# Attention and a ternary projection on one core: transposes of two units change places with slices of the projections

## The chip, the cores and the metric

The kernel runs on one core of a Trainium2 chip. The time is the device time in microseconds (us). The kernel before took 2060.3 us, the median of three runs (2057.4, 2060.3 and 2060.49). The profiled execution took 2057.48 us, of which the trace spans 2055.7 us.

The engines are named as in the profile: PE (the matrix engine, with its weight loads as PEld), DVE (the vector engine), ACT (the scalar engine), POOL (GpSimd) and SP (which issues the DMAs).

## The reference, cut to what matters

```python
# x: (8, 512, 1024) f32; 16 heads of 64; cond_1: (8, 1)
q, k, v = proj(x, Wq), proj(x, Wk), proj(x, Wv)       # (b, 16, 512, 64)
q = q * minimum(cond_1, 4.0)
scores = einsum('bhqd,bhkd->bhqk', q, k) / sqrt(64)
scores = where(causal, scores, finfo.min)
attn = softmax(scores)
out = einsum('bhqk,bhkd->bhqd', attn, v)
y = out.reshape(b, s, 1024) @ Wo.T
# ffn: weight rounded to -1, 0, 1 times alpha; y rounded to 8 bits by row
return x + absmax_act(y) @ ternary_weight(weight).T + bias
```

## The kernel before, in words

There are three stages. The first computes V for all batches (to about 345 us), the second does the attention (to about 1600 us), the last multiplies by Wo, quantises, and does the ternary product. The change lies in the second.

**Steps.** The 16 heads form 4 groups of 4. One step handles one batch and one group, so there are 32 steps, group by group, 8 batches each. A step projects Q and K of its 4 heads and does 16 units of attention: a unit u is one head and one tile of 128 queries (`h, qt = divmod(u, 4)`). By the causal mask the unit has only `(qt + 1) * 128` keys, so a unit is 128, 256, 384 or 512 wide in turn, and unit 5 has two 128-column blocks, unit 6 has three.

**The operands' precision.** Each f32 operand of the projections is kept as a high and a low part in fp32r. The x slices are split so: ACT writes the high part (`x_high`, L359), and the low part (`x_low`, L365) is computed by DVE for even slices k and by POOL for odd ones. A projection slice J(gi, k) is three matmuls of 512 columns (L174) and, for gi = 0, first waits until slice k's low part is there. gi is 0 to 3: K and Q of heads 0 and 1, then K and Q of heads 2 and 3.

**One unit's way.** S(u): two score matmuls on PE (L242, L243). M(u): DVE adds the mask and finds the row minimum (L254). E(u): ACT takes the exponential and the row sum (L261). I(u): DVE inverts the sum (L267). Then POOL normalises (L273). T(u): PE transposes `qt + 1` blocks into one of two `t_ps` banks (L283). H(u): ACT copies out the high part (L297). L(u): DVE the low part (L304). PV(h): eight matmuls with V for a head's four units (L317), which need the L of its last unit. T(u) waits for two things: that unit u is normalised, and that L(u - 2) has emptied its bank.

**The order.** Nothing is scheduled by a program: `pe_step`, `act_step`, `dve_step`, `pool_step` and `sp_step` each write out by hand what their engine does in a step. The attention of a step runs into the next: in these lists S(6) and later, and T(3) and later, are units of the step before (`old`), while J is of the present one (`now`). The head of a list is called a step's boundary here. There, ACT and DVE first empty the bank of the last projection, J(3) of the step before (`evac_hi`, `evac_lo`), and split the last x slices, 4 to 7. DVE does this in the order evac_lo(3), scale (L375), I(5), M(6), x_low 4, L(3), I(6), M(7), x_low 6, L(4), I(7). POOL does: normalise 5, x_low 5, normalise 6, normalise 7, x_low 7, normalise 8. ACT does H(6) directly ahead of V(0), the emptying of J(0)'s bank.

**Where old and now are both there.** This holds for 31 boundaries. In the first step there is no old, and after the last step there is no now.

**Group changes.** At three steps SP also loads the weights of the next group, behind the next x and ahead of the swapped copy of K, `k_sw` (L229, L230), that S(0) needs. In the step after each of these, ACT and DVE split one more piece of the weights at the boundary (L408, L398).

Of the kernel before, what the change touches and what calls it, by code (L numbers as in the profile page):

```python
# [36 lines left out]
def adaln_ffn_kernel(nc, x, xT, cond, wq, wk, wv, wo, wf, bias, out):  # L37
# [4 lines left out]
    with ExitStack() as ctx:  # L42
# [115 lines left out]
        def project(pe, it, g, gi, k):  # L158
            kind, n = groups[gi]
            bank = proj_ps[gi % 2]  # L160
            w = "kq".index(kind)
            if k == 0:

                if due(count := it * NEV + (EVAC[gi - 2] if gi >= 2 else EVAC[gi + NPROJ - 2] - NEV)):
                    pe.wait_ge(proj_lo_done, count)
                pe.wait_ge(wqk_lo_done, g * 4 + gi + 1)
            if gi == 0:
                pe.wait_ge(x_lo_done[k % 2], it * (KT // 2) + k // 2 + 1)
            col = slice(n * P, (n + 1) * P)
            out = bank[:, :]  # L170
            passes = [(w_lo[w][:, k, col], x_hi[:, k, :]), (w_hi[w][:, k, col], x_lo[:, k, :]),
                      (w_hi[w][:, k, col], x_hi[:, k, :])]
            for i, (l, r) in enumerate(passes):
                mm = pe.matmul(out, l, r, start=(k == 0 and i == 0), stop=(k == KT - 1 and i == 2))  # L174
            if gi == NPROJ - 1:

                mm.then_inc(x_free, 1)
            elif k == KT - 1:
                mm.then_inc(proj_done, 1)
# [52 lines left out]
        def scores(pe, it, u):  # L232
            h, qt = divmod(u, QT)
            n = it * UNITS + u
            if u % (2 * QT) == 0:
                pe.wait_ge(k_swapped[h // 2], (it + 1) * 32)
                pe.wait_ge(proj_lo_done, it * NEV + EVAC[h // 2 * 2 + 1])
            if due(count := n - 1):
                pe.wait_ge(max_done, count)
            w = (qt + 1) * P  # L240
            q = q_st[:, h, qt * P:(qt + 1) * P]
            pe.matmul(s_ps[u % 2][:, 0:w], q, k_sw[:, h, 0:w], start=True, stop=False)  # L242
            pe.matmul(s_ps[u % 2][:, 0:w], q, k_st[:, h, 0:w], start=False, stop=True).then_inc(s_done, 1)  # L243
# [32 lines left out]
        def transpose(pe, it, u):  # L276
            qt = u % QT
            n = it * UNITS + u
            pe.wait_ge(norm_done, n + 1)
            if due(count := n - 1):  # L280
                pe.wait_ge(pt_lo_done, count)
            for kb in range(qt + 1):
                mm = pe.transpose(t_ps[u % 2][:, kb * P:(kb + 1) * P], prob[:, u % 4, kb * P:(kb + 1) * P],  # L283
                                  ident[:, :])
            mm.then_inc(t_done, 1)
# [22 lines left out]
        def times_v(pe, it, h):  # L308

            pe.wait_ge(pt_lo_done, it * UNITS + (h + 1) * QT)  # L310
            pe.wait_ge(v_in[h], (it + 1) * 16)
            pe.wait_ge(o_sum_done[h % 2], it * NBLK + h // 2 + 1)
            for kb in range(QT):
                q0 = kb * P
                v = v_st[:, kb, h, :]
                for part in (pt_lo, pt_hi):
                    mm = pe.matmul(o_ps[h % 2][:, q0:S], v, part[h % 2][:, kb, q0:S],  # L317
                                   start=(kb == 0 and part is pt_lo), stop=(kb == QT - 1 and part is pt_hi))
            mm.then_inc(pv_done, 1)
# [172 lines left out]
        def attention_out(pe, t, p, half, k):  # L492
            first = isinstance(t, int) and t < 2
            if half == 0 and k == 0:
                pe.wait_ge(o_lo_done, t + 1)
                if not first:
                    if due(count := t - 1):
                        pe.wait_ge(y_free, count)
                elif t == 0:
                    pe.wait_ge(proj_lo_done, STEPS * NEV)  # L500
                else:
                    pe.wait_ge(max_done, STEPS * UNITS)
            if first and t == 0 and half == 0:
                pe.wait_ge(wo_lo_done, k + 1)
            w = slice(half * HALF, (half + 1) * HALF)
            o = slice(k * P, (k + 1) * P)
            for i, (a, b) in enumerate(((o_lo, wo_hi), (o_hi, wo_lo), (o_hi, wo_hi))):
                mm = pe.matmul(y_ps[p][half][:, :], a[p][:, o], b[k][:, w],  # L508
                               start=(k == 0 and i == 0), stop=(k == KT - 1 and i == 2))
            if k == KT - 1:  # L510
                mm.then_inc(y_done, 1)
# [674 lines left out]
        def pe_step(pe, old, now, nxt, qk_for=None, late_for=None, last=False):  # L1186
            o, n, g = old and old[0], now and now[0], now and now[1]

            def J(gi, *ks):
                if now:  # L1190
                    for k in ks:
                        project(pe, n, g, gi, k)

            def S(u):
                if u >= 6 and old:
                    scores(pe, o, u)
                elif u < 6 and now:
                    scores(pe, n, u)

            def T(u):  # L1200
                if u >= 3 and old:
                    transpose(pe, o, u)
                elif u < 3 and now:
                    transpose(pe, n, u)

            def PV(h):
                if old:
                    times_v(pe, o, h)

            def Y(t, half, *ks):  # L1210
                if last and not now:
                    for k in ks:
                        attention_out(pe, t, t, half, k)

            def YY(k):
                Y(0, 0, k)
                Y(0, 1, k)

            S(6)
            T(3)  # L1220
            J(0, 0, 1)
            YY(0)
            S(7)
            T(4)
            J(0, 2, 3)
            YY(1)
            S(8)
            T(5)
            J(0, 4, 5)
            PV(0)  # L1230
            J(0, 6)
            S(9)
            T(6)
            J(0, 7)
            J(1, 0)
            YY(2)
            S(10)
            T(7)
            J(1, 1, 2, 3)
            YY(3)  # L1240
            S(11)
            T(8)
            J(1, 4, 5)
            S(12)
            T(9)
            YY(4)
            PV(1)
            J(1, 6, 7)
            S(13)
            T(10)  # L1250
            J(2, 0, 1)
            YY(5)
            S(14)
            T(11)
            J(2, 2, 3)
            YY(6)
            S(15)
            T(12)
            J(2, 4, 5)
            if not old:  # L1260
                pe.wait_ge(v_sum_done, 4 * (PAIRS - PLAIN))
            S(0)
            T(13)
            YY(7)
            PV(2)
            J(2, 6)
            S(1)
            T(14)
            J(2, 7)
            J(3, 0)  # L1270
            Y(1, 0, 0, 1, 2)
            S(2)
            T(15)
            J(3, 1, 2)
            Y(1, 0, 3, 4)
            S(3)
            T(0)
            J(3, 3, 4)
            Y(1, 0, 5, 6, 7)
            S(4)  # L1280
            T(1)
            PV(3)
            J(3, 5, 6)
            S(5)
            T(2)
            J(3, 7)
# [329 lines left out]
        @block.tensor  # L1616
        def _(pe):
            v_pe(pe)
            pe.wait_ge(const_ready, CONSTS)
            program(pe, pe_step)  # L1620

            for k in range(KT):
                if k == KT // 2:
                    transpose_y(pe, 0, 0)
                attention_out(pe, 1, 1, 1, k)
            ternary(pe, 0, 0)

            def body(t, p):
                attention_out_half(pe, t, p, 0)
                transpose_y(pe, t - 1, 1 - p)  # L1630
                attention_out_half(pe, t, p, 1)
                ternary(pe, t - 1, 1 - p)

            pairs(pe, body)
            transpose_y(pe, TILES - 1, 1)
            ternary(pe, TILES - 1, 1)
# [81 lines left out]
```

## Time and profile before

| | |
|---|---|
| profiled execution | 2057.48 us |
| its span | 2055.7 us |
| median of three runs | 2060.3 us |
| PE busy | 1988.6 us (97%) |
| PEld busy | 1619.1 us (79%) |
| DVE busy | 1411.2 us (69%) |
| ACT busy | 1115.7 us (54%) |
| POOL busy | 872.2 us (42%) |

Busy is the time in which an engine had an operation under way. The matmuls overlap each other, so PE's share says how rarely it stood still and not how full it ran. In the attention stage a step takes 38.03 us in the steady part (from one q_scale operation to the next), and each boundary looks like the others to a few hundredths of a microsecond.

### The profile page before, as it was taken

Reading aid. Unit: us, or ns where it says so; the run is one execution under the profiler, and the core shown is the slowest. Engines: PE = TensorE matmul, PEld = TensorE weight load, DVE = VectorE, ACT = ScalarE, POOL = GpSimd, SP = SyncE. Lnnn points to the kernel's source line nnn. Section 1 sums busy time; section 2 is a strip of 40 time slices with the busy share of each in tenths; the row PEclk is TensorE's granted clock in tenths of the full one; section 3 lists DMA queues with packets and bytes.
Section 4 is the critical chain, followed back from the end, with each engine's and each line's share of the span. In section 5 each row is a group of like instructions: output and inputs, shape, how many; then the busy total and the mean of one; then the engine's idle time right before and its main releaser. Section 6 shows DMA issues by size and latency. Waiting matters only on the chain.

```text
span 2055.7 us, 34723 instructions
## 1 busy us (share of the span) xinstructions
PE 1988.6 (97%) x10074; PEld 1619.1 (79%) x10074; DVE 1411.2 (69%) x3277; ACT 1115.7 (54%) x2497; POOL 872.2 (42%) x816
## 2 busy tenths in 40 slices
PE   8999999999999999999999999999998999999998
PEld 6888887888877888877888877888886777777775
DVE  6667776777777777778777777777776645545454
ACT  4554445777777777777777777777774000000000
POOL 0344333444435444435445435445443544444442
PEclk9999999999999999999999999999999999999999
DMA  6676645533543533543533543533553432333322
GB/s 204 225 232 219 203 170 183 156 112 114 141 149 103 159 107 105 155 148 103 151 115 102 158 149 103 154 112 102 158 153 101 130 120 94 107 108 100 114 92 82
DMA packets 200981, 282.43 MB, mean 137 GB/s; under 512 B 11216, under 2 KB 146384, under 8 KB 199760
## 3 DMA queue, kind: packets, MB, share of 16 engines
q1 hardware_dynamic: 200384, 281.07, 44.9%
q8 instruction: 34, 0.56, 0.1%
q10 hardware_dynamic: 528, 0.52, 0.1%
q14 instruction: 35, 0.29, 0.0%
HBM read 178.79 MB, written 69.21 MB: 121 GB/s over the span
## 4 chain that ended last, share of the span: by engine, by line
PE 47%; issue 27%; POOL 15%; DVE 5%; DMA 3%; ACT 2%; SPq 1%; POOLq 1%; DVEq 0%; ACTq 0%
POOL prob L273 9%; PE proj_ps L508 8%; PE s_ps L508 8%; PE t_ps L869 7%; PE proj_ps L174 6%; PE o_ps L869 6%; POOL parts L365 5%; PE o_ps L579 5%; DMA k_sw<-k_st 2%; PE o_ps L317 1%; PE t_ps L283 1%; DVE prob L254 1%; DVE parts L365 1%; PE t_ps L557 1%; PE s_ps L808 1%
## 5 line engine op out<-in xcount | busy, mean ns | idle before, releaser
L174 PE MATMUL proj_ps<-parts 128*128 128x512 f32 x3072 | 839.2, 407 | 6.0 <-POOL parts L365 3.6
L273 POOL TENSOR_TENSOR prob<-prob,row_inv 128x128 f32<-128x128 f32 (+3 forms) x512 | 383.1, 748 | 693.5 <-DVE row_inv L267 690.9
L174 PEld LDWEIGHTS proj_ps<-parts 128*128 128x128 f32 x3072 | 538.8, 189 | 112.1 <-POOL parts L365 13.3
L261 ACT ACTIVATE prob<-prob,row_min 128x128 f32<-128x128 f32 (+3 forms) x512 | 287.5, 561 | 145.8 <-DVE row_min L254 139.5
L254 DVE CUSTOM_DVE_ANT_0 prob<-s_ps,mask 128x128 f32<-128x128 f32 (+3 forms) x512 | 248.2, 485 | 56.5 <-PE s_ps L243 22.1
L297 ACT ACTIVATE pt_hi<-t_ps 128x128 fp32r<-128x128 f32 (+3 forms) x512 | 220.7, 431 | 112.2 <-PE t_ps L283 108.2
L564 ACT ACTIVATE yt_q<-t_ps 128x1024 bf16<-128x1024 bf16 x32 | 32.7, 1023 | 427.1 <-PE t_ps L557 427.1
L304 DVE TENSOR_TENSOR pt_lo<-t_ps,pt_hi 128x128 fp32r<-128x128 f32 (+3 forms) x512 | 249.0, 486 | 16.7 <-ACT pt_hi L297 12.5
L283 PE MATMUL t_ps<-ident,prob 128*128 128x128 f32 x1280 | 227.4, 276 | 31.9 <-DVE pt_lo L304 29.4
L365 POOL TENSOR_TENSOR parts<-x_raw,parts 128x512 fp32r<-128x512 f32 x128 | 183.4, 1434 | 18.1 <-ACT parts L359 18.1
L508 PE MATMUL proj_ps<-parts,o_parts 128*128 128x512 f32 x768 | 188.2, 400 | 2.6 <-issue 2.6
L283 PEld LDWEIGHTS t_ps<-ident,prob 128*128 128x128 f32 x1280 | 152.7, 141 | 47.5 <-issue 34.2
L508 PE MATMUL s_ps<-parts,o_parts 128*128 128x512 f32 x768 | 185.6, 397 | 0.0
L508 PEld LDWEIGHTS proj_ps<-parts,o_parts 128*128 128x128 f32 x768 | 143.7, 190 | 33.6 <-issue 3.0
L508 PEld LDWEIGHTS s_ps<-parts,o_parts 128*128 128x128 f32 x768 | 143.2, 189 | 30.7
L243 PE MATMUL s_ps<-k_st,q_st 128*128 128x128 f32 (+3 forms) x512 | 166.0, 324 | 0.0
L242 PE MATMUL s_ps<-k_sw,q_st 128*128 128x128 f32 (+3 forms) x512 | 158.3, 309 | 7.2 <-DMA k_sw<-k_st 7.0
L317 PE MATMUL o_ps<-pt_lo,v_st 128*128 128x512 f32 (+3 forms) x512 | 161.6, 326 | 2.7 <-DVE pt_lo L304 2.7
L359 ACT ACTIVATE parts<-x_raw 128x512 fp32r<-128x512 f32 x256 | 152.0, 618 | 3.1 <-DMA x_raw<-xT 2.2
L317 PE MATMUL o_ps<-pt_hi,v_st 128*128 128x512 f32 (+3 forms) x512 | 147.7, 325 | 0.0
L267 DVE RECIPROCAL row_inv<-row_sum 128x1 f32<-128x1 f32 x512 | 82.5, 161 | 92.9 <-ACT prob L261 85.6
L334 DVE TENSOR_TENSOR o_sum<-o_ps,o_low 64x512 f32<-64x512 f32 x128 | 87.4, 683 | 82.6 <-ACT o_low L326 82.5
(118 smaller groups left out, 2880.3 us busy)
## 6 DMA issues: line engine op xcount, KB each, us to landing
x_raw<-xT SPq DMA_DIRECT2D x128, 512.0 KB, 5.7
v_scratch<-v_out SPq DMA_DIRECT2D x64, 512.0 KB, 3.3
k_sw<-k_st SPq DMA_DIRECT2D x128, 256.0 KB, 4.7
v_st<-v_scratch SPq DMA_DIRECT2D x128, 256.0 KB, 4.2
oT_scratch<-o_sum SPq DMA_DIRECT2D x64, 256.0 KB, 2.5
x_raw<-oT_scratch SPq DMA_DIRECT2D x32, 512.0 KB, 4.8
x_tile<-x SPq DMA_DIRECT2D x32, 512.0 KB, 5.4
out<-res SPq DMA_DIRECT2D x32, 512.0 KB, 3.2
```

What stands on the lines that cost most here:

```text
L174: mm = pe.matmul(out, l, r, start=(k == 0 and i == 0), stop=(k == KT - 1 and i == 2))
L243: pe.matmul(s_ps[u % 2][:, 0:w], q, k_st[:, h, 0:w], start=False, stop=True).then_inc(s_done, 1)
L254: dve.tensor_tensor_reduce(prob[:, u % 4, 0:w], s_ps[u % 2][:, 0:w], mask[:, S - w:S], 1.0, -MASKED, ALU.add, ALU.min, row_min[:, u % 4:u ...
L261: act.activation(prob[:, u % 4, 0:w], prob[:, u % 4, 0:w], ACT.Exp, bias=row_min[:, u % 4:u % 4 + 1], scale=-1.0, accum_out=row_sum[:, u % ...
L273: pool.tensor_tensor(prob[:, u % 4, 0:w], prob[:, u % 4, 0:w], row_inv[:, u % 4:u % 4 + 1].broadcast_to([P, w]), ALU.mult).then_inc(norm_d ...
L283: mm = pe.transpose(t_ps[u % 2][:, kb * P:(kb + 1) * P], prob[:, u % 4, kb * P:(kb + 1) * P], ident[:, :])
L297: act.activation(pt_view(pt_hi[h % 2], qt), t_ps[u % 2][:, 0:(qt + 1) * P] .rearrange("p (k q) -> p k q", q=P), ACT.Copy).then_inc(pt_hi_d ...
L304: dve.tensor_tensor(pt_view(pt_lo[h % 2], qt), t_ps[u % 2][:, 0:(qt + 1) * P] .rearrange("p (k q) -> p k q", q=P), pt_view(pt_hi[h % 2], q ...
L317: mm = pe.matmul(o_ps[h % 2][:, q0:S], v, part[h % 2][:, kb, q0:S], start=(kb == 0 and part is pt_lo), stop=(kb == QT - 1 and part is pt_hi))
L365: eng.tensor_tensor(x_lo[:, k, :], x_raw[:, k, :], x_hi[:, k, :].bitcast(F32), ALU.subtract).then_inc(x_lo_done[k % 2], 1)
L508: mm = pe.matmul(y_ps[p][half][:, :], a[p][:, o], b[k][:, w], start=(k == 0 and i == 0), stop=(k == KT - 1 and i == 2))
L869: mm = pe.matmul(bank[:, :], xv[:, c, xp, ks], wv_view(c, wp)[:, k, :], start=(k == 0 and m == 0 and c not in (S2, S3)), stop=(k == CH - 1 ...
```

## The change

In the order of PE's step, the transposes of unit 5 move behind the projection slice J(0, 4), and those of unit 6 behind J(0, 7). Nothing is added and nothing is left out. The order of the other engines is not touched.

```diff
             S(8)
+            J(0, 4)
             T(5)
-            J(0, 4, 5)
+            J(0, 5)
             PV(0)
             J(0, 6)
             S(9)
+            J(0, 7)
             T(6)
-            J(0, 7)
             J(1, 0)
             YY(2)
```

PE's order around T(5), in the loop over the batches: the two rows with s_ps are S(8), t_ps is T, proj_ps is J (three matmuls a slice), o_ps is PV(0). Before:

```order
L242 MATMUL s_ps<-k_sw,q_st 128x128
L243 MATMUL s_ps<-k_st,q_st 128x128
L283 MATMUL t_ps<-ident,prob 128x128 x2
L174 MATMUL proj_ps<-parts 128x512 x6
L317 MATMUL o_ps<-pt_lo,v_st 128x512
```

And now:

```order
L242 MATMUL s_ps<-k_sw,q_st 128x128
L243 MATMUL s_ps<-k_st,q_st 128x128
L174 MATMUL proj_ps<-parts 128x512 x3
L283 MATMUL t_ps<-ident,prob 128x128 x2
L174 MATMUL proj_ps<-parts 128x512 x3
L317 MATMUL o_ps<-pt_lo,v_st 128x512
```

The three matmuls of J(0, 4) stand ahead of the two transposes of T(5); those of J(0, 5) stay behind them.

PE's order around T(6): the first proj_ps row is J(0, 6), then S(9), T(6), and J(0, 7) with J(1, 0). Before:

```order
L174 MATMUL proj_ps<-parts 128x512 x3
L242 MATMUL s_ps<-k_sw,q_st 128x256
L243 MATMUL s_ps<-k_st,q_st 128x256
L283 MATMUL t_ps<-ident,prob 128x128 x3
L174 MATMUL proj_ps<-parts 128x512 x6
L242 MATMUL s_ps<-k_sw,q_st 128x384
```

And now:

```order
L174 MATMUL proj_ps<-parts 128x512 x3
L242 MATMUL s_ps<-k_sw,q_st 128x256
L243 MATMUL s_ps<-k_st,q_st 128x256
L174 MATMUL proj_ps<-parts 128x512 x3
L283 MATMUL t_ps<-ident,prob 128x128 x3
L174 MATMUL proj_ps<-parts 128x512 x3
L242 MATMUL s_ps<-k_sw,q_st 128x384
```

J(0, 7) stands ahead of the three transposes of T(6), J(1, 0) behind them.

## Rows read from the trace of the kernel before

**Rows 1.** PE's waits over the whole span: engine, line, waited for: us in total, times, longest.

```profile
PE t_ps L283 <- DVE pt_lo L304: 29.4, 35, 2.8
...
PE s_ps L242 <- DMA k_sw<-k_st: 7.0, 3, 2.4
PE proj_ps L174 <- POOL parts L365: 3.6, 3, 1.2
```

**Rows 2.** Timeline of PE at one boundary: start, duration, operation, count, [idle before <- releaser].

```profile
973.38 0.41 PE L283 MATMUL t_ps<-ident,prob 128*128 128x128 f32 x2 [0.86 <-DVE pt_lo L304]
973.55 1.64 PE L174 MATMUL proj_ps<-parts 128*128 128x512 f32 x6
...
976.98 0.28 PE L242 MATMUL s_ps<-k_sw,q_st 128*128 128x256 f32 x1
...
977.22 0.49 PE L283 MATMUL t_ps<-ident,prob 128*128 128x128 f32 x3
977.78 1.67 PE L174 MATMUL proj_ps<-parts 128*128 128x512 f32 x6
```

**Rows 3.** Timeline of DVE at the same boundary.

```profile
971.94 0.69 DVE L365 TENSOR_TENSOR parts<-x_raw,parts 128x512 fp32r<-128x512 f32 x1
972.55 0.68 DVE L304 TENSOR_TENSOR pt_lo<-t_ps,pt_hi 128x512 fp32r<-128x512 f32 x1
...
973.82 1.28 DVE L365 TENSOR_TENSOR parts<-x_raw,parts 128x512 fp32r<-128x512 f32 x1
...
975.22 0.15 DVE L267 RECIPROCAL row_inv<-row_sum 128x1 f32<-128x1 f32 x1
...
977.23 0.68 DVE L334 TENSOR_TENSOR o_sum<-o_ps,o_low 64x512 f32<-64x512 f32 x1 [0.94 <-ACT o_low L326]
```

**Rows 4.** Timeline of POOL at the same boundary.

```profile
971.99 1.77 POOL L365 TENSOR_TENSOR parts<-x_raw,parts 128x512 fp32r<-128x512 f32 x1
...
975.45 1.04 POOL L273 TENSOR_TENSOR prob<-prob,row_inv 128x512 f32<-128x512 f32 x1 [0.90 <-DVE row_inv L267]
976.44 1.28 POOL L365 TENSOR_TENSOR parts<-x_raw,parts 128x512 fp32r<-128x512 f32 x1
```

**Rows 5.** Timelines of ACT, POOL and PE, behind T(6).

```profile
977.75 0.49 ACT L297 ACTIVATE pt_hi<-t_ps 128x384 fp32r<-128x384 f32 x1 [0.64 <-PE t_ps L283]
978.87 1.21 ACT L210 ACTIVATE k_st<-proj_ps 64x512 fp32r<-64x512 f32 x2 [0.63 <-PE proj_ps L174]
...
981.18 0.61 POOL L273 TENSOR_TENSOR prob<-prob,row_inv 128x256 f32<-128x256 f32 x1 [3.10 <-DVE row_inv L267]
...
984.28 0.41 PE L283 MATMUL t_ps<-ident,prob 128*128 128x128 f32 x2
```

**Rows 6.** Timeline of PE where T(10) stands among projections, no waits.

```profile
987.42 0.49 PE L283 MATMUL t_ps<-ident,prob 128*128 128x128 f32 x3
987.67 1.63 PE L174 MATMUL proj_ps<-parts 128*128 128x512 f32 x6
```

**Rows 7.** Timeline of PE, J(0,7) at a boundary behind a change of group.

```profile
939.75 1.66 PE L174 MATMUL proj_ps<-parts 128*128 128x512 f32 x6 [1.20 <-POOL parts L365]
```

**Rows 8.** PE at two group changes; then one stretch, its PEclk third from the end.

```profile
913.81 0.33 PE L242 MATMUL s_ps<-k_sw,q_st 128*128 128x128 f32 x1 [2.35 <-DMA k_sw<-k_st]
...
922.01 0.39 PE L242 MATMUL s_ps<-k_sw,q_st 128*128 128x512 f32 x1
...
1223.68 0.33 PE L242 MATMUL s_ps<-k_sw,q_st 128*128 128x128 f32 x1 [2.24 <-DMA k_sw<-k_st]
...
1230.29 0.39 PE L242 MATMUL s_ps<-k_sw,q_st 128*128 128x512 f32 x1
...
915.50:917.00 1.50, 1.50 (x6) 1.31 (x6) 0.41 (x1) 0.59 (x1) 0.40 (x1) 0.50 0.00 1
```

**Rows 9.** Timeline of PE at the last boundary, T(6) and J(0,7).

```profile
1513.42 0.49 PE L283 MATMUL t_ps<-ident,prob 128*128 128x128 f32 x3
1514.02 1.66 PE L174 MATMUL proj_ps<-parts 128*128 128x512 f32 x6
```

## The prediction

> **What bounds the kernel now.** I first read the page's busy shares: PE has work under way for 97% of the span, so time can be won or lost only where PE stands still, or where it is given more or less to do. The change gives it the same instructions. So I then read PE's waits for the whole span [rows 1]. The largest is T waiting for the low part L, 29.4 us in 35 waits, nearly one for each of the 31 boundaries. Two smaller ones matter too: the swapped K that S(0) needs, three times and at most 2.4 us, and the x slice that POOL splits, three times.
>
> The third view is PE's timeline at one boundary, with those of DVE and POOL beside it [rows 2 to 4]. Here the reader is to see two stops on PE. The first is open: T(5) idles 0.86 us, until L(3) ends on DVE (972.55 + 0.68 = 973.23, and T(5) starts at 973.38). The second is nearly hidden. T(6) starts at 977.22, and the next slice, J(0,7), at 977.78, 0.56 us later. Where nothing is awaited, the same three transposes let the next slice start after 0.25 us (987.42 to 987.67) [rows 6]. J(0,7) therefore lost 0.31 us, and the row prints no idle for it only because the last transpose was still draining. What it waited for is x_low 7 on POOL, which ends at 976.44 + 1.28 = 977.72, 0.06 us before J(0,7) starts. I compared all 31 boundaries: POOL's end is followed by J(0,7) after 0.05 to 0.06 us in each. At the last one T(6) and J(0,7) are 0.60 us apart [rows 9].
>
> **The change part by part.** *T(5) behind J(0,4).* J(0,4) needs x_low 4, which DVE ends at 971.94 + 0.69 = 972.63, so with the same 0.06 us it starts at about 972.7. T(5) had been idle from 972.52. A slice takes half of the 1.47 us in which the six matmuls of a pair are issued, 0.73 us. J(0,4) is through at 973.4, when T(5) could start anyway. So J(0,4) costs nothing: it fills most of the hole. J(0,5) then waits for x_low 5, which POOL ends at 971.99 + 1.77 = 973.76. It starts at 973.82, where it started at 973.55 + 0.73 = 974.28 before. PE is 0.46 us ahead, and J(0,5), PV(0), J(0,6) and S(9) come that much earlier. That x_low 6 is ready for J(0,6) is seen from its end on DVE, 973.82 + 1.28 = 975.10, ahead of the end of PV(0).
>
> *J(0,7) ahead of T(6).* Now PE comes to J(0,7) where T(6) would have been, at 977.22 - 0.46 = 976.76, and J(0,7) needs x_low 7, which is ready at 977.72. Can the 0.46 us move x_low 7? Its chain is normalise 7 on POOL (from 975.45, released by DVE), behind I(7) on DVE (975.22), behind x_low 6 (973.82 to 975.10), behind L(3) and x_low 4 [rows 3, 4]. Every link of it is a DVE or POOL operation that waits for no instruction that PE now issues sooner; DVE works through it without a stop after the emptying of J(3). It begins with the end of J(3,7), which the change does not touch. So I take x_low 7 to stay at 977.72 and J(0,7) at 977.78, with about 1.02 us of idle in front of it. All that the first part won is given back here.
>
> What differs is what stands behind the wait. Before, T(6) ran inside the time that PE had to wait for x_low 7 anyway. Now it runs after it, between J(0,7) and J(1,0). Before, J(1,0) started at 977.78 + 0.73 = 978.51; now T(6) starts there and J(1,0) 0.25 us later. The cost is the 0.25 us of [rows 6]. Its bounds: T(5)'s two transposes let the next slice start after 0.17 us, so three cost at least 0.24 us when a block is 0.085; at most it is the 0.49 us for which a group of three is recorded. I take 0.25, the same count of the same form, and keep 0.35 as a practical upper end, an estimate for the extra break in the matmul stream.
>
> *What waits for the later T(6).* It starts at 978.51 and not at 977.22, 1.29 us later. H(6) on ACT goes from 977.75 to 979.04, and V(0), queued behind it, from 978.87 to about 979.5, 0.6 us later [rows 5]. On DVE L(6), the low part of J(0)'s bank, and then I(9) and M(10) follow 0.6 us later, and on POOL normalise 9 goes from 981.18 to 981.8, ending at 982.4. PE needs that for T(9) at 984.28. There are nearly 2 us of cover, so this costs nothing. The swapped K leaves 0.6 us later as well, but S(0), which needs it, stands in the second half of the step.
>
> *How often.* The boundary occurs 31 times. In three of them the step loads the next group's weights and S(0) then idles 2.24 to 2.40 us for the swapped K [rows 1, 8]. That transfer queues behind the x and weight loads, which start when x_low 7 is done and keep the DMA engines full, so it does not move. There PE's extra 0.25 us disappears into the idle time. Left are 28 times 0.25 = 7.0 us. On the profiled execution's own 2057.48 us that gives 2064.5, and on the median of 2060.3 it gives 2067.3. The profiled execution is at the fast end of the runs shown; I take 2066, between the two.
>
> *The clock.* It adds spread. At the first and second group change the granted clock fell after the idle time; one stretch behind it is at 0.50, the 1.2 GHz level. At the third, after 2.24 us idle, it did not fall. From S(0) to S(3) the second took 922.01 - 913.81 = 8.20 us and the third 1230.29 - 1223.68 = 6.61, so one fall costs 1.6 us [rows 8]. The change shortens this idle to 2.0 to 2.15 us, which could save the two falls, 3.2 us. But at the boundary behind a group change, J(0,7) idled 1.20 us behind T(6) [rows 7]. With T(6)'s recorded 0.49 and the 0.4 won before it, that becomes about 2.1 us. Three of these could fall, 4.8 us. I count both at nothing in the sum and give them to the range. The Trainium skill (TensorE: Matmul & The Clock Gate, "What's actually happening") says that a gate sets the clock by how busy PE has lately been. The two falls agree with that. By it, the change's one stop of 1 to 2 us is more exposed than the two shorter ones that it replaces.
>
> **The rivals.** *It does what its form suggests: faster.* If x_low 7 were not what J(0,7) waits for, or moved forward with PE, J(0,7) would start at 976.76, J(1,0) at 976.76 + 0.73 + 0.25 = 977.74 instead of 978.51. That is 0.77 us, 28 times, 21.6 us: 2036 on the own time, 2039 on the median. It breaks even when x_low 7 ends 0.25 us earlier. For it speaks the 0.86 us idle at T(5), which J(0,4) really fills; against it, the 0.06 us between POOL's end and J(0,7), 31 times. 6%.
>
> *No difference.* The 7 us are there, but the shorter wait at the group changes keeps the clock up at two of them (-3.2), and nothing falls elsewhere: 2061.3 on the own time, 3.8 above it, which is inside what a measurement tells from nothing (0.2%, 4.1 us). Or some later wait that I read as zero takes up the 0.25 us. For it: the 2.24 us that passed without a fall. Against: J(0,7)'s 2.1 us has the same length. 12%.
>
> *Clearly slower.* POOL's x_low took 1.77 us in x_low 5 and 1.28 in x_low 7; during the former DVE's x_low 4 ran, which reads SBUF twice. Now OA(0) and M(9) move 0.46 us forward into x_low 7. If they slowed it by the same 0.49 us, J(0,7) would be later by that: 28 times 0.49 = 13.7 more, 2078 on the own time. Against it: OA(0) already ran beside x_low 7 (from 977.23 on) before, and x_low 7 took only its 1.28 us; OA(0) reads one of its inputs from PSUM. The Trainium skill (GPSIMD Engine Reference, "Key points") says that POOL shares SBUF interfaces with DVE and contends with instructions that have two SBUF inputs. By that rule x_low 4 slows POOL and OA(0) does not, as the rows have it. 5%.
>
> *My forecast,* 0.25 us in each of 28 steps, with falls of the clock going either way: 77%.
>
> **How the numbers follow.** Predicted 2066. The low end: the own time, 28 times 0.24 = 6.7, less 3.2 for two falls saved, 2061; I go to 2060 to take in part of the second rival. The high end: 2060.3, 28 times 0.35 = 9.8, and 4.8 for three new falls, 2074.9; I stop at 2074. The rest of the chance is outside. Slower by over 0.2%: the forecast and the third rival, 82%. Within 0.2%: 12%. Faster: 6%.
>
> **What would show it.** In the changed kernel's trace, T(5)'s wait for L(3) has gone or is below 0.1 us, and J(0,4) stands in its place. J(0,7) idles about 1.0 us, released by POOL's x_low, in 31 boundaries, so PE's waits show some 30 us there where they show 3.6 now. From the start of J(0,7) to J(1,0) it takes about 0.98 us, and a steady step 38.28 us and not 38.03. I am wrong if x_low 7 ends closer to J(3,7) than before, if the step is shorter than 38.0, or if a wait of PE appears that is in neither list, above all at T(9) or PV(1).

## The result, and the profile after

The changed kernel took 2069.84 us, the median of five runs (2066.54 to 2070.87), against 2060.3 us before. The ratio is 1.0045, with a 95% interval of 1.003 to 1.006. It is slower by 0.3 to 0.6%, as forecast, by 9.5 us where 7 were forecast on the median. The profiled execution spans 2068.1 us against 2055.7.

PE's waits over the whole span, after the change (to be laid beside [rows 1]):

```profile
PE proj_ps L174 <- POOL parts L365: 27.9, 31, 1.9
...
PE s_ps L242 <- DMA k_sw<-k_st: 7.1, 3, 2.9
PE t_ps L283 <- DVE pt_lo L304: 5.6, 5, 2.7
PE proj_ps L174 <- DVE parts L365: 3.8, 23, 0.2
```

The two large waits have changed places. T's wait for the low part fell from 29.4 to 5.6 us. The wait for the x slice that POOL splits rose from 3.6 to 27.9 us and now shows at all 31 boundaries. Together they are 33.5 us where they were 33.0. The last row is new: it is J(0,4), which now waits for x_low 4. All three together grew by 4.3 us, and the span by 12.4, so the printed waits alone do not explain the loss.

PE's timeline at an ordinary boundary, after (the answer to [rows 2]):

```profile
1015.02 0.97 PE L174 MATMUL proj_ps<-parts 128*128 128x512 f32 x3 [0.17 <-DVE parts L365]
1015.83 0.38 PE L283 MATMUL t_ps<-ident,prob 128*128 128x128 f32 x2
1016.17 0.96 PE L174 MATMUL proj_ps<-parts 128*128 128x512 f32 x3
...
1018.94 0.28 PE L242 MATMUL s_ps<-k_sw,q_st 128*128 128x256 f32 x1
1019.05 0.28 PE L243 MATMUL s_ps<-k_st,q_st 128*128 128x256 f32 x1
1020.13 0.96 PE L174 MATMUL proj_ps<-parts 128*128 128x512 f32 x3 [0.79 <-POOL parts L365]
1020.93 0.49 PE L283 MATMUL t_ps<-ident,prob 128*128 128x128 f32 x3
1021.17 0.95 PE L174 MATMUL proj_ps<-parts 128*128 128x512 f32 x3
1021.96 0.33 PE L242 MATMUL s_ps<-k_sw,q_st 128*128 128x384 f32 x1
```

J(0,4) fills the hole in front of T(5). Then J(0,7) stands still for POOL, and T(6), which used to run inside that wait, runs behind it. From the start of J(0,7) to S(10) it is 1.83 us (1020.13 to 1021.96).

POOL at the same boundary, and DVE's q_scale operation there and one step on (the answer to [rows 4], and the length of a step). The last row is q_scale before the change, at the boundary of [rows 2 to 5]:

```profile
1017.80 1.04 POOL L273 TENSOR_TENSOR prob<-prob,row_inv 128x512 f32<-128x512 f32 x1 [0.90 <-DVE row_inv L267]
1018.80 1.27 POOL L365 TENSOR_TENSOR parts<-x_raw,parts 128x512 fp32r<-128x512 f32 x1
...
1013.39 0.15 DVE L375 TENSOR_SCALAR q_scale<-cond_bc 128x1 f32 x1
...
1051.80 0.15 DVE L375 TENSOR_SCALAR q_scale<-cond_bc 128x1 f32 x1
...
971.06 0.15 DVE L375 TENSOR_SCALAR q_scale<-cond_bc 128x1 f32 x1
```

x_low 7 ends at 1018.80 + 1.27 = 1020.07, 6.68 us after q_scale, where it ended 6.66 us after it before (977.72 - 971.06). PE was 0.4 us ahead at S(9), and POOL did not move. The step from one q_scale to the next is 38.41 us here and 38.35 to 38.41 in the others of the steady part; before it was 38.03. In the profile the 24 ordinary intervals are longer by 0.35 us each, 8.5 of the 12.4 us. Three intervals behind a group change add 1.1, the first boundary 0.3. The remaining 2.4 us lie in the group changes (1.1) and behind the last q_scale (1.3), where the clock fell at other places than before (see the eighth experiment).

T(6) comes later, and so do the operations that wait for it, at no cost. ACT and POOL behind it, and PE's T(9) (the answers to [rows 5]):

```profile
1021.45 0.49 ACT L297 ACTIVATE pt_hi<-t_ps 128x384 fp32r<-128x384 f32 x1 [2.38 <-PE t_ps L283]
1021.84 1.20 ACT L210 ACTIVATE k_st<-proj_ps 64x512 fp32r<-64x512 f32 x2
...
1024.25 0.61 POOL L273 TENSOR_TENSOR prob<-prob,row_inv 128x256 f32<-128x256 f32 x1 [3.82 <-DVE row_inv L267]
...
1026.97 0.41 PE L283 MATMUL t_ps<-ident,prob 128*128 128x128 f32 x2
```

H(6) starts 8.06 us after q_scale and started 6.69 after it before. Normalise 9 is 0.74 us later, ends at 1024.86, and T(9) starts at 1026.97 without a wait.

### The profile page after: what moved, and what is told of

Read it like the earlier page. It is cut to its first block, busy times and chain, and to the rows that moved or that the text cites. A ratio compares the mean times of both kernels' runs of the same rounds, so it can differ in the third digit from the quotient of the medians.

```text
span 2068.1 us, 34723 instructions
## 1 busy us (share of the span) xinstructions
PE 1998.1 (97%) x10074; PEld 1619.0 (78%) x10074; DVE 1409.5 (68%) x3277; ACT 1111.9 (54%) x2497; POOL 872.2 (42%) x816
## 4 chain that ended last, share of the span: by engine, by line
PE 46%; issue 27%; POOL 15%; DVE 5%; DMA 3%; ACT 2%; POOLq 1%; SPq 0%; DVEq 0%; ACTq 0%
POOL prob L273 9%; PE proj_ps L508 8%; PE s_ps L508 8%; PE t_ps L869 7%; PE proj_ps L174 6%; POOL parts L365 5%; PE o_ps L579 5%; PE o_ps L869 5%; DMA k_sw<-k_st 2%; PE o_ps L317 1%; PE t_ps L283 1%; DVE prob L254 1%; DVE parts L365 1%; PE t_ps L557 1%; PE s_ps L808 1%
## 5 line engine op out<-in xcount | busy, mean ns | idle before, releaser
L174 PE MATMUL proj_ps<-parts 128*128 128x512 f32 x3072 | 857.0, 410 | 31.8 <-POOL parts L365 27.9
```

## The experiments

Four kernels ran on one chip beside the kernel before (the first to fourth below), then four more. A ratio is that of the kernel's runs to those of before on its chip, with its 95% interval. The length of a step is read from the q_scale rows of the steady part.

**1. The first half alone.**

```diff
             S(8)
+            J(0, 4)
             T(5)
-            J(0, 4, 5)
+            J(0, 5)
```

> Only the first half of the change: J(0,4) stands ahead of T(5); T(6) stays ahead of J(0,7). Theory A (J(0,7) starts when POOL's x_low 7 is done, whatever PE won before): PE is 0.46 us ahead up to T(6), waits longer at J(0,7), J(0,7) starts 6.72 us after q_scale as before, the steady step stays 38.03 us, the time within 0.1% of before. Rival B (PE's own stops are what a step loses, x_low 7 moves with PE): the step is 0.4 us shorter, about 12 us in all, ratio 0.994. Rival C (the loss of the full change comes from splitting J(0,4) and J(0,5), a restart of 0.1 us): the step is 0.1 us longer, +3 us.

Measured: 2061.14 us, ratio 1.0004 (0.9995 to 1.0013), step 38.03 us. Theory A. Its PE timeline from J(0,4) to J(0,7):

```profile
1011.92 0.96 PE L174 MATMUL proj_ps<-parts 128*128 128x512 f32 x3 [0.17 <-DVE parts L365]
1012.72 0.38 PE L283 MATMUL t_ps<-ident,prob 128*128 128x128 f32 x2
...
1016.08 0.49 PE L283 MATMUL t_ps<-ident,prob 128*128 128x128 f32 x3
1017.04 1.66 PE L174 MATMUL proj_ps<-parts 128*128 128x512 f32 x6 [0.47 <-POOL parts L365]
1018.54 0.33 PE L242 MATMUL s_ps<-k_sw,q_st 128*128 128x384 f32 x1
```

Before, T(6) and J(0,7) were 0.56 us apart; here they are 0.96 us apart. The 0.4 us that PE won at T(5) is all there, as a longer wait. This half removed 25 us from the line of PE's largest wait and made the kernel no faster.

**2. The second half alone.**

```diff
             S(9)
+            J(0, 7)
             T(6)
-            J(0, 7)
             J(1, 0)
```

> Only the second half of the change: J(0,7) stands ahead of T(6); T(5) as before, with its 0.86 us of waiting. Theory A: the whole loss is here. J(0,7) starts 6.72 us after q_scale, T(6) and a new start of the matmul run come behind it, the step is 38.38 us as with the full change, 28 steps by 0.35 us = +10 us, ratio 1.0045 to 1.005. Rival B (the loss is shared between the halves, or the first half's gain hides some of it): half of it, +5 us, or more than the full change's, above +13 us.

Measured: 2066.24 us, ratio 1.0026 (1.0016 to 1.0036), step 38.36 us. The step is within 0.03 us of that of the full change, so all but 0.03 us of the steady loss is in this half. The time is 6 us above before, between the two theories' numbers, and the steps decide: they add 0.33 us each. Why the totals of this kernel and the full change differ by more than their steps is for the eighth experiment.

**3. x_low 7 earlier, PE's order as before.**

```diff
             for u in range(5, UNITS):
+                if now and old and u == 7:
+                    x_low(pool, n, u)
                 if old:
                     normalise(pool, o, u)
-                if now and old and u in (5, 7):
+                if now and old and u == 5:
                     x_low(pool, n, u)
```

> PE's order as before; on POOL the low part of x slice 7 goes ahead of normalise 7 and not behind it. Theory A: x_low 7 starts when ACT has written its high part, some 1.1 us earlier (about 975.4 and not 976.4 on the time axis of the boundary shown), J(0,7) follows T(6) after 0.25 us and not 0.56 to 0.6, the steady step is 37.7 us, and the steps behind a group change win 1.4 us. 28 by 0.31 plus 3 by 1.1 = 12 us faster, ratio 0.994. The wait of T(5) is unchanged at 0.86 us. Rival B (x_low 7 does not bind, or normalise 7, now 0.3 to 1.3 us later, becomes what T(7) waits for): no change, or slower, with a wait at T(7).

Measured: 2040.43 us, ratio 0.9908 (0.9892 to 0.9923), step 37.70 us. POOL and PE in it:

```profile
999.91 0.82 POOL L273 TENSOR_TENSOR prob<-prob,row_inv 128x384 f32<-128x384 f32 x1
1001.53 1.29 POOL L365 TENSOR_TENSOR parts<-x_raw,parts 128x512 fp32r<-128x512 f32 x1 [0.80 <-ACT parts L359]
1002.78 1.40 POOL L273 TENSOR_TENSOR prob<-prob,row_inv 128x512 f32<-128x512 f32 x2
```

```profile
1003.39 0.49 PE L283 MATMUL t_ps<-ident,prob 128*128 128x128 f32 x3
1003.64 1.64 PE L174 MATMUL proj_ps<-parts 128*128 128x512 f32 x6
```

x_low 7 now follows ACT's high part, 1.1 us earlier, and J(0,7) follows T(6) after 0.25 us. That x_low 7 was the bound is shown by this. The step came out to the hundredth, but the total gained 20 us and not 12. My sum had left out the three steps of a group change. SP starts the loads there when x_low 7 is done: at the first, 6.7 us after q_scale before and 5.6 here, and S(0)'s three idle times for the swapped K went from 2.40, 2.35 and 2.24 us to 1.70, 2.08 and 1.96. Those three intervals went from 42.87, 42.81 and 41.13 us to 40.21, 40.57 and 40.45. Part of that is the clock: before, it fell in the first two of them, and here in none. At the 1.6 us of [rows 8] for a fall, an estimate, that is 3.2 of the 5.6 us; the third interval, without a fall in either kernel, is 0.7 us shorter. Whether the shorter idle time kept the clock up, or chance did, is not shown. The intervals behind them went from 39.05 to 37.6, not by the 1.1 I had put.

**4. T(6) beside T(7),** with T(5) where it was before.

```diff
             S(9)
-            T(6)
             J(0, 7)
             J(1, 0)
             YY(2)
             S(10)
+            T(6)
             T(7)
```

> PE's T(6) stands still later: behind J(0,7), J(1,0) and S(10), directly ahead of T(7); T(5) as before. So T(6) again comes behind the wait for x_low 7 but no run of projection matmuls is split. If the 0.35 us of the full change are 0.25 for three transposes and 0.1 for a new start of the matmul run behind them, the step is 38.28 us, +7 us, ratio 1.0034. If three transposes cost 0.35 wherever they stand, 38.38 us, +10 us. If the lateness of T(6) is what costs (H(6), queued ahead of V(0) on ACT, is 2 us later here), more than that: waits appear at T(8) or T(9), above +12 us.

Measured: 2065.52 us, ratio 1.0024 (1.0014 to 1.0034), step 38.35 us. Its PE timeline:

```profile
1020.80 1.66 PE L174 MATMUL proj_ps<-parts 128*128 128x512 f32 x6 [0.41 <-POOL parts L365]
1022.29 0.34 PE L242 MATMUL s_ps<-k_sw,q_st 128*128 128x384 f32 x1
1022.47 0.34 PE L243 MATMUL s_ps<-k_st,q_st 128*128 128x384 f32 x1
1022.65 0.93 PE L283 MATMUL t_ps<-ident,prob 128*128 128x128 f32 x7
1023.33 2.30 PE L174 MATMUL proj_ps<-parts 128*128 128x512 f32 x9
```

No run of projections is split and T(6) stands among other transposes. The kernel to lay it beside is that of the second experiment, which also leaves T(5) in its old place: its step is 38.36 us, within 0.01 of this one. Seven transposes take 0.68 us from their first start to the next slice. In the changed kernel the four of T(7) alone take 0.35 us:

```profile
1022.31 0.60 PE L283 MATMUL t_ps<-ident,prob 128*128 128x128 f32 x4
1022.66 1.64 PE L174 MATMUL proj_ps<-parts 128*128 128x512 f32 x6
```

So three more cost 0.33 us, 0.11 each, wherever they stand. The idea of 0.25 for the transposes and 0.1 for the restart of the run falls; the split itself costs 0.01 us at most here. T(6) is 2.4 us later in the step than before here, and no wait appeared at T(8) or T(9), so its lateness was not the cost either.

**5. The full change with the earlier x_low 7** (the change's diff and that of the third experiment).

> The full change, with POOL's x_low 7 ahead of normalise 7. If x_low 7 was what kept the change from winning, then now J(0,7) starts right behind S(9), 5.8 us after q_scale, J(1,0) at 6.8, and the steady step is 37.35 to 37.4 us, 0.3 shorter than with the earlier x_low 7 alone (37.70). In the steps behind a group change x_low 7 ends at 6.24 and J(0,7) still waits 0.4 us there with T(6) behind it. 31 by 0.3 = 9 us under the 2040 us of the earlier x_low 7 alone: about 2031, ratio 0.986. Rival: T(6), 0.4 us later than there, or the first half's waits for x_low 5 eat it, and the time stays at 2040.

Measured: 2032.92 us, ratio 0.9874 (0.9859 to 0.989), step 37.33 us. PE in it:

```profile
998.25 0.28 PE L243 MATMUL s_ps<-k_st,q_st 128*128 128x256 f32 x1
998.37 0.87 PE L174 MATMUL proj_ps<-parts 128*128 128x512 f32 x3
999.08 0.49 PE L283 MATMUL t_ps<-ident,prob 128*128 128x128 f32 x3
```

J(0,7) starts 0.12 us behind S(9), with no wait. The very edit that lost 7 to 10 us gains 7.5 us over the third experiment's kernel once x_low 7 is out of the way (9 were expected).

**6. The first half with the earlier x_low 7.**

> The first half of the change alone (J(0,4) ahead of T(5)), with the earlier x_low 7. The 0.37 us that the first half put PE ahead at T(6), and which were given back at J(0,7), now stay: steady step 37.33 us, no wait at J(0,7) in it, 31 by 0.37 = 11.5 us under 2040: about 2029, ratio 0.985. The second half of the change is then worth nothing or a loss: the full change with the earlier x_low 7 is 1 to 3 us slower than this. Rival: the two edits do not add, 2040.

Measured: 2031.86 us, ratio 0.9863 (0.9848 to 0.9878), step 37.28 us. The edits add in the step, which gave its 0.4 us. The gain is 8.6 us over the third experiment where I had put 11.5. The profiled execution, the slowest of the four (2034.99 us), has longer group-change intervals (41.9, 41.9 and 42.1 us, where the third experiment's kernel had 40.2 to 40.6), and its clock fell in all three of them and in none of the other's. So falls of the clock hide part of the gain there; how many there were in the other executions is not known. The second half of the change is again no gain: the step is 0.05 us longer with it, which is the price of T(6) between J(0,7) and J(1,0) where nothing waits, and behind a group change, where J(0,7) still waits for x_low 7, 0.36 us longer (37.93 against 37.57). In the medians the two are 1 us apart, which their intervals do not tell from nothing.

**7. And J(0,5) behind PV(0).**

```diff
             S(8)
+            J(0, 4)
             T(5)
-            J(0, 4, 5)
             PV(0)
+            J(0, 5)
             J(0, 6)
```

(with the third experiment's diff)

> As the kernel with the first half and the earlier x_low 7, but J(0,5) stands behind PV(0): J(0,4), T(5), PV(0), J(0,5), J(0,6). J(0,5) waits 0.17 us for x_low 5 where it stands now; PV(0) needs only L(3), which T(5) has awaited. 31 by 0.17 = 5 us less than that kernel, about 2024, ratio 0.9825. Rival: PV(0) behind the transposes costs as much as it saves, no change.

Measured: 2025.24 us, ratio 0.9834 (0.982 to 0.9848), step 37.09 us. PE in it:

```profile
993.05 0.38 PE L283 MATMUL t_ps<-ident,prob 128*128 128x128 f32 x2
993.19 0.48 PE L317 MATMUL o_ps<-pt_lo,v_st 128*128 128x512 f32 x1
...
994.50 1.61 PE L174 MATMUL proj_ps<-parts 128*128 128x512 f32 x6
```

PV(0) runs right behind T(5), and the pair J(0,5), J(0,6) behind it waits for nothing. It gains 6.6 us over the sixth experiment where 5 were expected. This is the fastest version, 35 us (1.7%) under the kernel before.

**8. The changed kernel once more.**

> The changed kernel itself, once more. The second half alone gave 2066.2 us with a steady step of 38.37 us, the full change 2069.8 with 38.39. If the first half really costs nothing in time, the full change runs within 2 us of 2067; if it costs something beyond the steady step, 2069 to 2071 again.

Measured: 2066.87 us (2061.72 to 2067.64), ratio 1.0038 (1.0024 to 1.0051), step 38.38 us. That agrees with the second half alone. The profiled execution spans only 2059.9 us, 8.2 us less than the other execution of the same program. The stretch about the first group change in the first execution, and the same stretch in this one (the third number from the end is the granted clock):

```profile
580.00:625.00 45.00, 41.74 (x212) 34.60 (x212) 34.56 (x91) 32.80 (x77) 18.87 (x22) 0.96 0.49 157
```

```profile
580.00:625.00 45.00, 42.31 (x222) 34.92 (x221) 36.61 (x95) 35.00 (x81) 20.56 (x23) 1.00 0.48 159
```

Its clock was at 1.000 over the whole span, against 0.996. The first had it fall at two group changes and about the start of the last stage. The group-change intervals make 5.2 us of the 8.2, the time behind the last q_scale 3.5, and the rest goes the other way by 0.6. The steady steps are the same in both, 38.35 to 38.42 us. The 8 us between two executions of one program are thus as large as the effect, and the 3 us by which the full change and its second half differ need no cause beyond that spread; the runs do not exclude a small one.

## Why the prediction was right, and where it was off

**What J(0,7) waits for.** Right, and shown from both sides. Winning time ahead of it changed nothing (experiment 1); moving x_low 7 alone won 0.33 us in each step and 20 us in all, the clock's part included (experiment 3). The forecast place of x_low 7, unmoved by PE's lead, holds to 0.02 us.

**The first half gives back all it wins.** Right: 0.4 us of lead was forecast as 0.46, and the kernel with that half alone is level with before. J(0,4) did fill the hole at T(5), behind a wait of 0.17 us for x_low 4 (972.52 to 972.7 in the working), and J(0,5) starts when x_low 5 is done, as worked out.

**The price of T(6) behind the wait.** The mechanism was right, the size too small: 0.25 us was forecast for a step and 0.35 measured. The misread term is the row pair at T(10) [rows 6], from the start of three transposes to the start of the next slice. That is not what a group costs, since the first matmul behind it is followed by the next only after more than the usual time. The first three matmuls of J behind T(10), one by one, in the kernel before:

```profile
987.67 0.48 PE L174 MATMUL proj_ps<-parts 128*128 128x512 f32 x1
...
987.99 0.39 PE L174 MATMUL proj_ps<-parts 128*128 128x512 f32 x1
...
988.21 0.39 PE L174 MATMUL proj_ps<-parts 128*128 128x512 f32 x1
```

The second starts 0.32 us behind the first, where later ones are 0.23 us apart. The 0.25 us plus these 0.09 is 0.34, which the fourth experiment confirms by another way (0.33). The 1.47 us of a pair hold the same 0.09 once, and I had halved them unseen. I had named 0.35 as an end for "an extra break in the stream"; the number was right and the reason wrong, as the break costs 0.01 us where J(0,7) waits (experiments 2 and 4) and 0.05 where it does not (experiments 5 and 6). With 0.35 the sum is 28 times 0.35 = 9.8 us, against 9.5 and 7.0 us measured in the two comparisons (medians 2069.84 and 2066.87, less 2060.3 and 2059.91).

**Cover for the late T(6).** Right. Normalise 9 was 0.74 us later where 0.6 was forecast, with 2.1 us left ahead of T(9). No wait appeared at T(9) or PV(1); the one new row among PE's waits is J(0,4)'s, which lies ahead of the wait for x_low 7 and is absorbed in it.

**Group changes.** That the swapped K would hide the loss in three steps could not be read from the totals, as a fall of the clock moves such a step by 1.6 us: the three intervals changed by -0.1, -1.3 and +2.5 us. In the second execution, with no fall of the clock, they were 40.57, 40.99 and 41.23 us. Like laid beside like, the first interval, with a fall in both kernels, changed by -0.1 us, and the third, without one before and in the second execution after, by +0.1. That fits a hidden loss, but the three intervals of the second execution differ by 0.7 among themselves, so it stays open. Behind a group change J(0,7) idled 1.91 us, and the feared fall of the clock did not come there in any of the three. The rule of the Trainium skill (TensorE: Matmul & The Clock Gate, "What's actually happening") that the gate follows how busy PE has lately been was of no use to tell one from the other: over the ten traces, group changes with a fall had PE idle for 1.98 to 3.50 us ahead of S(0), those without for 1.34 to 2.66.

**Rivals.** "Faster" failed on its condition, and experiment 5 shows that it was stated rightly: with x_low 7 early the same edit does win. "Clearly slower" by a slowed x_low 7 is excluded: OA(0) and M(9) came forward, and x_low 7 took 1.27 us after and 1.28 before. The Trainium skill (GPSIMD Engine Reference, "Key points") names DVE instructions with two SBUF inputs, or in a 2-port mode, as those that contend with POOL. OA(0) and M(9) have one of theirs in PSUM, and the trace agrees. The other side of the rule can be seen in the third experiment's kernel, behind a group change, where x_low 7 runs beside a weight split of DVE that reads SBUF twice. There it took 1.73 us, and 1.29 at the other boundaries:

```profile
621.25 1.21 DVE L398 TENSOR_TENSOR parts<-w_raw,parts 128x1024 fp32r<-128x1024 f32 x1
...
621.90 1.73 POOL L365 TENSOR_TENSOR parts<-x_raw,parts 128x512 fp32r<-128x512 f32 x1 [1.11 <-ACT parts L359]
```

## What to carry to other kernels

A stop that is filled with useful work gains nothing if a later stop at the same kind of boundary waits for another engine's chain; look first for the last wait before the loop closes, also where its row shows no idle because a pipelined operation still drains. Work that stands inside a wait is free, and behind it has its full price, so keep what is ready ahead of the instruction that waits. Here one operation moved on POOL, which the profile showed 42% busy, was worth 20 us, and the reorderings of the busiest engine that were tried gained 8.6 and 6.6 us on top of it; the first of the two, tried without it, gained nothing.

## What the runs showed of the hardware

A group of three or more 128-column f32 transposes among 512-column fp32r matmuls costs 0.11 us for each transpose, and part of it shows in the gap behind the first matmul that follows (0.32 us and not 0.23). And two profiled executions of one program spanned 2068.1 and 2059.9 us with the granted clock at 0.996 and 1.000. One fall of the clock behind a stop of 2.35 us costs 1.6 us [rows 8], and whether it comes differs from one execution to the next.

Where two operations of DVE and POOL both read SBUF, the one that started second was the longer. In the kernel before, POOL's x_low 5 starts 0.05 us behind DVE's x_low 4 and takes 1.77 us, where x_low 7 takes 1.28. DVE's x_low 4, the first to start, takes 0.69 us. Its x_low 6, the same operation, takes 1.28 us [rows 3]: it starts 0.10 us behind POOL's normalise 6, which is this row:

```profile
973.72 0.82 POOL L273 TENSOR_TENSOR prob<-prob,row_inv 128x384 f32<-128x384 f32 x1
```
